# Grouped-query attention: probabilities and values split into high and low parts, weighed in three single passes

## The reference

```python
q = _rms_norm(q, q_norm_w)
k = _rms_norm(k, k_norm_w)
q, k = _apply_rope(q, k, cos, sin)
k = jnp.repeat(k, groups, axis=1)
v = jnp.repeat(v, groups, axis=1)
scores = jnp.einsum('bhqd,bhkd->bhqk', q, k) * scaling
scores = jnp.where(causal[None, None], scores, jnp.finfo(scores.dtype).min)
attn = jax.nn.softmax(scores.astype(jnp.float32), axis=-1).astype(q.dtype)
out = jnp.einsum('bhqk,bhkd->bhqd', attn, v)
out = jnp.transpose(out, (0, 2, 1, 3)).reshape(b, s, NH * HD)
return out @ Wo
```

## Time and profile before

| | |
|---|---|
| median of 3 runs | 1942.68 us (1942.01 to 1944.75) |
| the profiled execution's own time | 1947.12 us |
| its span, first to last instruction | 1945.3 us |
| mean granted TensorE clock | 0.906 of full speed |
| busy: PE, PEld | 1580.6 us (81%), 1161.8 us (60%) |
| busy: DVE, ACT, POOL | 1103.1 us (57%), 910.6 us (47%), 711.9 us (37%) |
| L1479, weighing, x768 instructions | 272.1 us busy |
| L1200, copies of chunks, x384 | 174.4 us busy, 490 ns mean |

### The profile page before, as it was taken

The page is one execution under the profiler, slowest core; times in us unless marked ns, Lnnn a source line. Parts: engine busy times, 40 slices in busy tenths (PEclk is TensorE's granted clock), DMA queues, the critical chain, the costliest instruction groups (busy, mean ns, idle before and its releaser), DMA issues. The chain is left out here.

```text
span 1945.3 us, 27408 instructions
## 1 busy us (share of the span) xinstructions
PE 1580.6 (81%) x9258; PEld 1161.8 (60%) x9258; DVE 1103.1 (57%) x2141; ACT 910.6 (47%) x1925; POOL 711.9 (37%) x700
## 2 busy tenths in 40 slices
PE   6899789779864663837999999999999999998373
PEld 4444578668752222725776677767777677776262
DVE  4665354665458985446555555566455655554533
ACT  2365334234424323425555566555655565564342
POOL 3011260415044747046434343444343444420603
PEclk9899799888987995868999999999999999999586
DMA  3321324213324004430000000000000000000443
GB/s 76 52 50 50 110 100 126 76 50 113 125 61 174 0 10 158 144 114 14 10 17 12 6 12 17 9 9 12 12 7 12 12 9 12 7 7 3 161 141 103
DMA packets 80214, 106.57 MB, mean 55 GB/s; under 512 B 12336, under 2 KB 64176, under 8 KB 79696
## 3 DMA queue, kind: packets, MB, share of 16 engines
q1 hardware_dynamic: 73936, 88.04, 15.2%
q0 software_dynamic: 6144, 16.79, 2.7%
HBM read 70.64 MB, written 27.72 MB: 51 GB/s over the span
## 5 line engine op out<-in xcount | busy, mean ns | idle before, releaser
L1307 DVE TENSOR_SCALAR_CACHE_REDUCE gqa_scaled<-acc,gqa_neg_scale 128x128 bf16<-128x128 f32 (+7 forms) x256 | 208.9, 816 | 312.6 <-PE acc L1459 311.2
L1479 PE MATMUL aux<-gqa_probsT,gqa_v 128*128 128x512 f32 (+3 forms) x768 | 272.1, 491 | 11.2 <-DVE gqa_turned_k L1263 7.0
L1200 ACT ACTIVATE gqa_probsT<-aux 128x512 f32<-128x512 f32 (+3 forms) x384 | 174.4, 490 | 188.1 <-PE aux L1470 188.1
L1190 ACT ACTIVATE gqa_probs<-acc,gqa_bias,gqa_q_scale 128x128 f32<-128x128 f32 (+7 forms) x256 | 213.5, 834 | 46.7 <-DVE gqa_scaled L1307 40.3
L1084 POOL TENSOR_TENSOR gqa_q_high<-gqa_straight,gqa_turned_q 128x512 fp32r<-128x512 f32 x64 | 87.8, 1371 | 327.5 <-DVE gqa_turned_q L1263 327.5
L1479 PEld LDWEIGHTS aux<-gqa_probsT,gqa_v 128*128 128x128 f32 x768 | 138.2, 190 | 103.0 <-issue 62.1
L1470 PE MATMUL aux<-ident,gqa_probs 128*128 128x128 f32 x1152 | 168.9, 274 | 0.3 <-ACT gqa_probsT L1200 0.3
L1458 PE MATMUL acc<-gqa_k_high,gqa_q_high 128*128 128x512 f32 (+3 forms) x384 | 156.7, 408 | 7.2 <-DVE gqa_k_low L1291 5.7
L1458 PE MATMUL acc<-gqa_k_high,gqa_q_low 128*128 128x512 f32 (+3 forms) x384 | 133.5, 348 | 0.0
L1458 PE MATMUL acc<-gqa_k_low,gqa_q_high 128*128 128x512 f32 (+3 forms) x384 | 133.0, 346 | 0.0
L1470 PEld LDWEIGHTS aux<-ident,gqa_probs 128*128 128x128 f32 x1152 | 124.6, 141 | 0.6 <-issue 0.4
(11 more groups left out here) (417 smaller groups left out, 4284.0 us busy)
## 6 DMA issues: line engine op xcount, KB each, us to landing
f_w<-in_f_up SPq DMA_DIRECT2D x64, 256.0 KB, 2.8
f_xs<-tokens_by_slot SPq DMA_DIRECT2D x108, 128.0 KB, 2.2
outputs_by_slot<-f_y_tile SPq DMA_DIRECT2D x108, 128.0 KB, 1.7
f_w<-in_f_down SPq DMA_DIRECT2D x64, 128.0 KB, 2.9
mat_qk<-mat_high SPq DMA_DIRECT2D x64, 64.0 KB, 2.3
scan_b_all<-scan_rows SPq DMA_DIRECT2D x1, 4096.0 KB, 21.0
gqa_w_q<-in_g_wq SPq DMA_DIRECT2D x32, 128.0 KB, 2.1
gqa_wo<-in_g_wo SPq DMA_DIRECT2D x32, 128.0 KB, 2.0
```

The costliest lines, as they stand in the source:

```text
L1190: act.activation(probs_of(t, 0, t + 1), scores(t), ACT.Exp, bias=bias[:, n % 16:n % 16 + 1], scale=q_scale[:, h // 2 % 2, h % 2 * NT + t:h ...
L1200: act.activation(turned_tile(t, a, b), aux[:, chunk(n, c) % 2, 0:(b - a) * P].rearrange("p (s w) -> p s w", w=P), ACT.Copy).then_inc(chunk ...
L1307: dve.tensor_scalar(scaled[:, 0:width(t)], scores(t), neg_scale[:, h // 2 % 2, h % 2 * NT + t:h % 2 * NT + t + 1], None, ALU.mult, ALU.min ...
L1479: last = pe.matmul(weigh_bank(half)[:, first:], v[:, h // GQ % 2, s, :], moving, start=s == 0, stop=s == 4 * half + 3)
```

## The change

The turned probabilities and the values are kept as high and low parts in fp32r. ScalarE's copies, which wrote `probsT` and `v`, now write the high parts; VectorE subtracts these from the same PSUM banks to make the low parts (`low_chunks`, 12 instructions a head, and `low_v`, 16 in all). Each weighing matmul becomes three on fp32r operands. A chunk's bank is now free, and the weighing may start, when the low part is made and no longer when the copy is done; the bank of `kv` likewise. To make room, `probs` keeps four tiles in place of eight, and `k_square` two in bf16, for which ScalarE waits on its own earlier squares. (L and line numbers in the rows of the order below are those of each kernel.)

```diff
-        v = sb("v", [P, 2, NT, HD])
+        v_high = sb("v_high", [P, 2, NT, HD], F32R)
+        v_low = sb("v_low", [P, 2, NT, HD], F32R)
-        probs = sb("probs", [P, P * NT * (NT + 1) // 2])
-        probsT = sb("probsT", [P, 2 * STAIRS + 4 * FULL])
+        probs = sb("probs", [P, 26 * P])
+        probsT_high = sb("probsT_high", [P, 2 * STAIRS + 4 * FULL], F32R)
+        probsT_low = sb("probsT_low", [P, 2 * STAIRS + 4 * FULL], F32R)
...
-                act.activation(v[:, g % 2, 2 * q:2 * q + 2, :], bank[:, :, 1, :], ACT.Copy).then_inc(v_copied, 1)
+                act.activation(v_high[:, g % 2, 2 * q:2 * q + 2, :], bank[:, :, 1, :], ACT.Copy).then_inc(v_copied, 1)
...
-                    act.activation(turned_tile(t, a, b), aux[:, chunk(n, c) % 2, 0:(b - a) * P].rearrange("p (s w) -> p s w", w=P),
+                    act.activation(turned_tile(probsT_high, t, a, b), aux[:, chunk(n, c) % 2, 0:(b - a) * P].rearrange("p (s w) -> p s w", w=P),
...
+            def low_v(g, q):
+                dve.wait_ge(v_copied, 4 * g + q + 1)
+                bank = kv_bank(g, q).rearrange("p (t w d) -> p t w d", w=2, d=HD)
+                pair = slice(2 * q, 2 * q + 2)
+                dve.tensor_tensor(v_low[:, g % 2, pair, :], bank[:, :, 1, :], v_high[:, g % 2, pair, :].bitcast(F32),
+                                  ALU.subtract).then_inc(v_low_ready, 1)
+
+            def low_chunks(n):
+                t = n % NT
+                for c, (a, b) in enumerate(parts(t)):
+                    dve.wait_ge(chunk_copied, chunk(n, c) + 1)
+                    dve.tensor_tensor(turned_tile(probsT_low, t, a, b),
+                                      aux[:, chunk(n, c) % 2, 0:(b - a) * P].rearrange("p (s w) -> p s w", w=P),
+                                      turned_tile(probsT_high, t, a, b).bitcast(F32), ALU.subtract).then_inc(chunk_low_ready, 1)
...
                 if n < STEPS:
                     row_max(n)
+                if 0 <= n - TURN < STEPS:
+                    low_chunks(n - TURN)
                 if j == 1 and h >= 1:
                     invert(h - 1, 1)
                     low_oT(h - 1, 0)
...
+                    if kv_step(n):
+                        low_v(*kv_step(n))
...
                 elif kind == "kv":
-                    pe.wait_ge(v_copied, 4 * a + b + 1)
+                    pe.wait_ge(v_low_ready, 4 * a + b + 1)
...
                     if chunk(n, c) >= 2:
-                        pe.wait_ge(chunk_copied, chunk(n, c) - 1)
+                        pe.wait_ge(chunk_low_ready, chunk(n, c) - 1)
...
-                    pe.wait_ge(chunk_copied, CHUNKS_OF_HEAD * h + (CHUNKS_OF_HEAD if half else 4))
+                    pe.wait_ge(chunk_low_ready, CHUNKS_OF_HEAD * h + (CHUNKS_OF_HEAD if half else 4))
                 for s in keys:
-                    first, moving = turned_keys(half, s)
-                    last = pe.matmul(weigh_bank(half)[:, first:], v[:, h // GQ % 2, s, :], moving, start=s == 0, stop=s == 4 * half + 3)
+                    first, high = turned_keys(probsT_high, half, s)
+                    _, low = turned_keys(probsT_low, half, s)
+                    for m, (left, right) in enumerate(three(v_high[:, h // GQ % 2, s, :], v_low[:, h // GQ % 2, s, :], high, low)):
+                        last = pe.matmul(weigh_bank(half)[:, first:], left, right, start=s + m == 0, stop=(s, m) == (4 * half + 3, 2))
```

More of the change, by code:

```diff
@@ L827, in gqa_layer @@
         k_tokens = sb("k_tokens", [P, NT, HD])
-        k_square = sb("k_square", [P, NT, HD])
+        k_square = sb("k_square", [P, 2, HD], BF16)
         turned_k = sb("turned_k", [P, HALF])
@@ L896, in gqa_layer @@
         chunk_copied = sem("chunk_copied")
+        chunk_low_ready = sem("chunk_low_ready")
+        v_low_ready = sem("v_low_ready")
         pv_done = sem("pv_done")
@@ L914, in probs_of @@
         def probs_of(t, a, b):
-            first = P * t * (t + 1) // 2
+            first = P * (0, 5, 11, 18)[t % 4]
             return probs[:, first + a * P:first + b * P]
@@ L924, in chunk, with turned_tile @@
             return CHUNKS_OF_HEAD * (n // NT) + CHUNKS[n % NT] + c
-        def turned_tile(t, a, b):
+        def turned_tile(probsT, t, a, b):
             at = t % 4 * P
@@ L932, in turned_tile, with turned_keys @@
             return probsT[:, at:at + (b - a) * STAIR].rearrange("p (s w) -> p s w", w=STAIR)[:, :, 0:P]
-        def turned_keys(half, s):
+        def turned_keys(probsT, half, s):
             if half and s < 4:
@@ L1170, in key_values @@
                 for t in range(2):
-                    act.activation(k_square[:, 2 * q + t, :], bank[:, t, 0, :], ACT.Square,
+                    if NT * g + 2 * q >= 2:
+                        act.wait_ge(k_squared, NT * g + 2 * q + t - 1)
+                    act.activation(k_square[:, t, :], bank[:, t, 0, :], ACT.Square,
                                    accum_out=k_scale[:, g, 2 * q + t:2 * q + t + 1]).then_inc(k_squared, 1)
                 act.activation(k_tokens[:, 2 * q:2 * q + 2, :], bank[:, :, 0, :], ACT.Copy).then_inc(k_copied, 1)
-                act.activation(v[:, g % 2, 2 * q:2 * q + 2, :], bank[:, :, 1, :], ACT.Copy).then_inc(v_copied, 1)
+                act.activation(v_high[:, g % 2, 2 * q:2 * q + 2, :], bank[:, :, 1, :], ACT.Copy).then_inc(v_copied, 1)
             def high_k(g, c):
@@ L1334, in _ @@
             rope(0, 1)
+            for q in range(4):
+                low_v(0, q)
             key_mean(0)
@@ L1501, in _ @@
             pe.wait_ge(v_copied, 4)
+            pe.wait_ge(v_low_ready, 4)
             turn_k(0, 0)
```

## The result

The changed kernel took **2047.17 us** (median of 3 runs, 2045.74 to 2051.01): 1.0532 times the kernel before, 95% interval 1.0512 to 1.0552. The forecast was 2050 (2010 to 2090). All times are medians of undisturbed executions; one execution in the second experiment took 7070 us where its others took 2077 to 2081, and is left out.

A forecast was written before the change was run, and what follows sets the result against it. The prediction took TensorE and VectorE to be geared together at four points per head, with little or no slack. Plain heads at 1.84 + 1.1 + 0.94 - 1.15 = +2.7 us, plus other heads, gave +108 us: 2050 us (2010 to 2090).

The forecast's parts named there:

- three points: Places in a head where low parts stand ahead of VectorE work that TensorE needs: +1.84, +1.1 and +0.94 us.
- other chunks: Low parts of tiles 0 to 3 and 5 fall where VectorE waits for scores: no cost in even heads.
- Saving: Weighing on TensorE: three fp32r passes in place of fp32 take 1.15 us less per head (0.55 to 1.65).
- First point: Tile 6's low parts ahead of `low_oT` delay the output projection `out(h-1, 0)` by 1.84 us (1.65 to 2.0).
- Second point: Tile 7's low parts ahead of the adds delay `project(h+2, 1)` by 1.1 us (0.8 to 1.4).
- Third point: Tile 4's low parts ahead of `add(h-1, 2)` delay the first half's weighing by 0.94 us (0.7 to 1.2).
- Sum: Plain head +2.7 us, odd heads +1.0 more, `kv` steps +0.7, heads 30 and 31 +2.9 each; whole kernel +108 us.
- Clock: Rival: 2 us stops lower TensorE's clock in some heads; five such heads cost +100 us, 2150 us; chance 0.04.
- No change: Rival: the stops just eat the saving, about 1943 us; chance 0.03.
- VectorE as bound: Rival: waits in VectorE's queue add an uncovered link, such as 1.5 us of narrower chunks, 2098 us; chance 0.10.
- Low parts in the idle time: Rival: low parts vanish in VectorE's idle time, only TensorE's saving counts, 1909 us; chance 0.06.
- Signs: Expected in the trace: VectorE busy near 78%, three TensorE waits for it near 4 us a head, even period near 27.9.

The follow-up runs named there:

- second experiment: Changed kernel with all low parts and waits, but each weighing is one plain fp32 matmul on the high parts: 2077.46 us.
- Kernel 1: Changed kernel without the low parts of the probabilities on VectorE; the third matmul takes the high part again: 1921.92 us.
- Kernel 3: Changed kernel with `invert` and `low_oT` moved ahead of tile 6's low parts in VectorE's queue: 2020.57 us.
- kernel 4: Kernel 1 plus subtractions of the low parts' sizes and places on VectorE, from two always-ready SBUF operands, nobody waiting for results: 2103.42 us.
- kernel 5: Changed kernel with queues relaid: VectorE serves the points before the low parts, TensorE projects the first half ahead of the turn: 1946.77 us.
- kernel 6: The kernel before, without the split, in the queue layout of kernel 5: 1956.86 us.
- kernel 7: kernel 5 with query weights split at step 3 in place of 7 and their low part made earlier on GpSimd: 1902.77 us.
- kernel 8: The kernel before, without the split, in the layout of kernel 7 with the query weights early: 1905.35 us.
- kernel 9: kernel 7 with VectorE's low parts at step 0 put ahead of `rope`: 1913.40 us.

## Why the prediction was right, point by point

The steps of one plain even head (28), in us, each from the start of the last matmul of a tile's score to that of the next tile's, show price and saving apart. Kernel 1 has the saving without the low parts, so what the changed kernel takes above it is the price:

| step after the score of tile | 0 | 1 | 2 | 3 | 4 | 5 | 6 | 7 |
|---|---|---|---|---|---|---|---|---|
| before | 4.83 | 1.36 | 3.64 | 3.42 | 3.92 | 3.78 | 2.62 | 1.60 |
| kernel 1 | 4.56 | 1.36 | 3.63 | 3.26 | 3.40 | 3.55 | 2.66 | 1.63 |
| changed | 5.35 | 1.36 | 5.36 | 4.31 | 3.40 | 3.55 | 2.67 | 1.63 |

Three steps pay, those of the three points, and the other five are the same within 0.01 us. The low parts of the other chunks cost nothing here, as the prediction said.

- **Saving, 1.15 us a head.** Right in the plain even head, 1.13 (kernel 1). The single passes start 0.23 us apart for 512 columns, and 0.18, 0.12 and 0.11 for 384, 256 and 128, so the 36 matmuls take some 6.6 us (6.7 forecast). An estimate from the four passes of true fp32 in the Trainium skill, FP8 and Floating Point Precision, TensorE Precision Notes, would have had a quarter saved, 0.55 of the first half's 2.18 us; 0.20 was measured. The trace agrees with the four passes as far as it goes: the two instructions of an fp32 matmul on 512 columns started 0.43 us apart, so it took 0.86, near four times the 0.23 of a single pass. But three single passes take 0.69, a fifth less and not a quarter, and on 128 columns nothing is saved, since a pass there costs nearly as much as one on 256. The prediction's own reason, that its rows make narrow passes dearer per column, doesn't hold: 0.17 us for 384 columns is the same per column as 0.23 for 512, and it is only at 128 that the pass gets dear. As a sum over 32 heads, 37 us, the term was too large: 22 were measured, for the waits named under kernel 1.
- **First point, +1.84.** `low_oT` came 2.23 us after the row maximum (2.3 forecast), TensorE's wait is 1.66, and the step behind tile 2 grew by 1.73 us. Kernel 3 shows that the place is the cause.
- **Second point, +1.1.** The wait is 0.78 us, and the step behind tile 3 takes 1.05 us more than in kernel 1; against the kernel before it is 0.89, because this step also holds 0.16 of the saving.
- **Third point, +0.94.** The adds came 0.80 us later, and the step behind tile 0 takes 0.79 us more than in kernel 1. One thing was put wrongly: the turn of tile 5 was to end sooner than the adds. It waits 0.45 us for the low parts of tile 4, and the weighing starts right behind it; adds and turn end together, so the price is the same by either.
- **Sum.** Plain even heads 27.64 (27.9 forecast); odd heads grew by 0.77 more than their neighbours (+1.0); head 30 +2.84 (+2.9). At `kv` the even head grew by 2.95 us, 0.49 more than a plain one (+0.7). The whole came to +104 us, forecast +108. The price alone, 133 us, and the saving, 22, are both smaller than the forecast's 145 and 37. The two errors offset each other, so the whole came closer than its terms: that part is luck.
- **Rivals.** *Clock:* in the changed kernel the granted clock stayed 1.00 from the second head on, in 1600 to 1700 us at 85.21 us busy. What the rival described did come where single stops were longer, in kernels 4, 5 and 6. *No change:* refuted, for the three points cost three times the saving. *VectorE as bound:* refuted by kernels 5 and 7, which do all of its work. *Low parts in the idle time:* refuted for this order, and true of the other: with the points served first they cost no more than they save (kernels 7 and 8).
- **Signs.** VectorE busy 73.11%, not 78%: I divided by the even period, where even and odd heads average 29 us, which explains three of the five points. The three waits named as near 4 us a head make 49.9 + 21.9 + 8.5 us and smaller ones, some 3; the rest of the loss stood at `kv` and `sum_squares`.

## What to carry to other kernels

Before work is put on an engine that "has room", ask at each point where the bound engine takes something from it how long that was ready; where the answer is nothing, as at the points here, an instruction put ahead of it costs about its full length. Where the work stands can be worth more than how much it is: here 144 us lie between two orders of the same work, of which the layout gave 40 without the split too. When work is moved earlier, go through all that it reads, the weights prepared on other engines included: in kernels 5 and 9 the next wait was one that nobody had on the list. And run the old kernel in the new layout before a gain is put down to the change.

## What the hardware showed unexpectedly

A subtraction of 512 columns took 686 ns on VectorE with one operand in PSUM and one in SBUF, and 1013 ns on average in kernel 4 with both in SBUF. On kernel 4's timeline it is seen where:

```profile
1776.42 1.29 POOL L1088 TENSOR_TENSOR gqa_q_high<-gqa_straight,gqa_turned_q 128x512 fp32r<-128x512 f32 x1 [7.61 <-DVE gqa_turned_q L1269]
...
1776.85 3.08 DVE L1312 TENSOR_TENSOR gqa_probsT_low<-xnT 128x512 fp32r<-128x512 f32 x2
1777.67 1.70 POOL L1089 TENSOR_TENSOR gqa_straight<-gqa_straight,gqa_turned_q 128x512 f32<-128x512 f32 x1
1779.52 1.53 POOL L1092 TENSOR_TENSOR gqa_q_low<-gqa_straight,gqa_q_high 128x512 fp32r<-128x512 f32 x1
1779.85 1.26 DVE L1347 SCALAR_TENSOR_TENSOR stream<-aux,gqa_row_inv,stream 128x256 f32<-128x256 f32 x3
```

While GpSimd runs its three query instructions, two subtractions take 3.08 us, and the second and third of GpSimd's own take 1.70 and 1.53 where their medians in the changed kernel are 1.28 and 1.29. Two operands in SBUF are not slow by themselves: of the 192 stand-ins of 512 columns, the 96 that ran while GpSimd ran nothing took 680 to 690 ns, as the real low parts did, and the other 96 took 1278 ns on average. The Trainium skill, SBUF — State Buffer, section Who interferes with whom, says that a VectorE instruction with two SBUF inputs contends with a GpSimd instruction that reads SBUF, because its second input comes through a read interface that the two share; the trace agrees, with 1278 against 687 ns. So a stand-in for a cost must have its operands in the same memories as what it stands for.
